# Attention products on four 32-row strips: float32r parts in place of bf16 parts, four products handed out at a time

## The reference, cut to what matters

```python
# first attention: keys and values from a stride-2 depthwise convolution over the tokens
q = x @ q_w.T + q_b                       # 512 rows
xd = conv(x, stride 2) + conv_b           # 256 rows
k = xd @ k_w.T + k_b; v = xd @ v_w.T + v_b
att = softmax(einsum('bhnd,bhmd->bhnm', q, k) * scale)
out = einsum('bhnm,bhmd->bhnd', att, v)
...
# the others, 512 by 512
att = einsum('bhqd,bhkd->bhqk', q, k) / np.sqrt(D)
att = jnp.where(causal, att, -jnp.inf)
att = softmax(att); out = einsum('bhqk,bhkd->bhqd', att, v)
```

## Time and profile before

| | |
|---|---|
| median of 3 runs | 1876.41 us (1875.72 to 1876.76) |
| profiled execution, span from first to last instruction | 1910.5 us |
| time of the profiled execution around its span | not recorded |
| PE / DVE / ACT / POOL busy | 81% / 68% / 51% / 56% of the span |
| attention block that is not causal (units 0 to 31) | about 140 to 410 us |
| causal block of 8 batches | about 546 to 843 us in full swing |
| causal block of 16 batches | about 1064 to 1690 us |

### The profile page before, as it was taken

One profiled execution on the slowest core, in us unless ns is written; L12 is line 12 of the kernel. 1 busy time (PEld: TensorE's weight loads), 2 busy tenths in 40 slices (PEclk: granted clock), 3 DMA queues, 4 the chain that ended last, 5 costly groups with the idle time before them and its releaser, 6 DMA issues. The chain is left out here.

```text
span 1910.5 us, 46442 instructions
## 1 busy us (share of the span) xinstructions
PE 1556.0 (81%) x17682; PEld 947.9 (50%) x17682; DVE 1307.4 (68%) x3414; ACT 968.9 (51%) x2039; POOL 1077.0 (56%) x1712
## 2 busy tenths in 40 slices
PE   5548888885599998885899499999999999866992
PEld 5432333344355554543677255555555555435772
DVE  7348897883588887766321588888888787775224
ACT  4124667652256676552233166777777766531331
POOL 3436767514467857654354376465566767552552
PEclk9966999987689999886799599999999999975996
DMA  8442323212533222210353343233232223102445
GB/s 279 128 127 86 109 70 95 78 30 83 146 99 115 91 82 78 88 36 22 99 152 102 117 128 105 79 94 103 79 114 82 83 92 103 47 26 62 148 123 160
DMA packets 233187, 188.24 MB, mean 99 GB/s; under 512 B 30035, under 2 KB 221306, under 8 KB 232326
## 3 DMA queue, kind: packets, MB, share of 16 engines
q1 hardware_dynamic: 222582, 166.36, 29.1%
q0 software_dynamic: 10240, 18.89, 3.1%
q10 hardware_dynamic: 144, 0.00, 0.0%
HBM read 104.34 MB, written 80.74 MB: 97 GB/s over the span
## 5 line engine op out<-in xcount | busy, mean ns | idle before, releaser
L1015 DVE TENSOR_REDUCE mx<-PS 128x2 f32<-128x512 f32 (+3 forms) x1408 | 784.3, 612 | 193.2 <-PE PS L653 138.2
L865 ACT ACTIVATE pt<-PS 128x512 f32<-128x512 f32 (+2 forms) x1408 | 669.6, 537 | 311.5 <-PE PS L653 227.9
L670 PE MATMUL PS<-ka,qa 52*128 52x256 bf16 (+3 forms) x2048 | 467.0, 307 | 67.1 <-DVE mx L1015 49.3
L786 PE MATMUL PS<-qa,ka 55*128 55x512 bf16 (+3 forms) x1792 | 462.2, 322 | 33.6 <-DMA qa<-nm 26.5
L730 PE MATMUL PS<-pt,vs 128*32 128x512 f32 (+3 forms) x3584 | 353.1, 484 | 3.7 <-issue 3.0
L653 PE MATMUL PS<-mask_q,identh 64*128 64x64 bf16 x3072 | 301.3, 193 | 0.7 <-issue 0.7
L653 PE MATMUL PS<-mask_k,identh 64*128 64x64 bf16 x3072 | 299.6, 192 | 0.5 <-issue 0.5
L786 PEld LDWEIGHTS PS<-qa,ka 55*128 55x128 bf16 x1792 | 167.6, 94 | 262.6 <-issue 102.7
L653 PEld LDWEIGHTS PS<-mask_k,identh 64*128 64x128 bf16 x3072 | 250.2, 97 | 51.1 <-issue 6.6
L653 PEld LDWEIGHTS PS<-mask_q,identh 64*128 64x128 bf16 x3072 | 254.3, 98 | 30.2 <-issue 8.2
L670 PEld LDWEIGHTS PS<-ka,qa 52*128 52x128 bf16 x2048 | 172.8, 95 | 98.1 <-DVE mx L1015 61.2
(11 more groups left out here) (249 smaller groups left out, 2353.2 us busy)
## 6 DMA issues: line engine op xcount, KB each, us to landing
pt<-in_f_w SPq DMA_DIRECT2D x96, 256.0 KB
qa<-q_parts SPq DMA_DIRECT2D x256, 96.0 KB
ka<-k_parts SPq DMA_DIRECT2D x192, 96.0 KB
q_parts<-parts SPq DMA_DIRECT2D x32, 384.0 KB, 3.0
k_parts<-parts SPq DMA_DIRECT2D x24, 384.0 KB, 2.6
xn<-y_rows SPq DMA_DIRECT2D x32, 256.0 KB, 3.2
hid<-y_rows SPq DMA_DIRECT2D x32, 256.0 KB, 3.5
q_parts<-parts SPq DMA_DIRECT2D x32, 256.0 KB, 3.1
```

The source lines that it names most:

```text
L670: mm = pe.matmul(PS[:, bank, i * n:(i + 1) * n], k.qa[rows, b % 2, g, h // 2, qb * P:(qb + 1) * P], k.ka[rows, b % 2, g, h // 2, 0:n], sta ...
L786: mm = pe.matmul(PS[:, bank, i * n:(i + 1) * n], k.ka[rows, b % 2, g, h // 2, kb * P:(kb + 1) * P], k.qa[rows, b % 2, g, h // 2, q0:S], st ...
L865: nc.scalar.activation(k.pt[:, u % 2, at[c]:at[c] + len(heads) * n], PS[:, SC_BANK + c % RING, 0:len(heads) * n], ACT.Exp, scale=SCORE_SCA ...
L1015: nc.vector.tensor_reduce(out, PS[:, MX_BANK + t % RING, 0:len(heads) * n] .rearrange("p (h n) -> p h n", n=n), AX.X, ALU.max).then_inc(s. ...
```

## The change

- Parts: queries and keys are split into two parts, the first rounded to float32r and the second the rest in float32. Three products of parts are summed. With a spare row for each feature that makes 4 times 8 = 32 rows, one strip of the array, one head a strip. The negative maximum goes into two of the spare rows, in two parts, so `put_max` has two DMAs and `max_split` two POOL steps where there were four; `split` has two where there were four. All four heads of a unit sit on the four strips of one tile.
- Hand-out: `slots` issues two score tiles and two max tiles together, on four different strips, after their waits; then second pieces, and then their masks, strip by strip. Its semaphore increments come with the last mask.
- Masks: a diagonal square gets four 32-row products of 32 columns, 64 on each side in a unit (32 before), in bf16 as before. The step rows are gone.
- Tiles: a causal unit still has 12 and 12. The score tiles are 4 of 512, 4 of 384 and 4 of 256 + 128 columns of one head; the max tiles are 4 of 512, 4 of 384 + 128 and 4 of 256. The 384 + 128 tile is reduced in blocks of 128, so one small reduction per unit is added on DVE, and `max_T` waits for it (`mx_ready`).
- Order: inserted work stands behind odd slots alone, `max_T` and `nm` behind slot 1, `value_p` behind slot 3, and the others are dealt out anew.
- The loads of a unit are one DMA for queries and one for keys (two each before), 32-bit data in rows of 2 KB.

```diff
-NPROD = 6
-Q_ROWS = (slice(0, 6, 2), slice(1, 6, 4), slice(3, 4))
-K_ROWS = (slice(3, 6), slice(1, 3), slice(0, 1))
...
+STRIP = P // HG
+DROWS = STRIP // D
+Q_ROWS = (slice(0, 3, 2), slice(1, 2))
+K_ROWS = (slice(1, 3), slice(0, 1))
+SPARE = 3
+MAX_ROWS = (SPARE, SPARE + DROWS)
+WRITES = 2
+MASKS = P // STRIP
...
-        chunks = ([(0, (h,), 512) for h in (0, 1, 2, 3)] + [(1, (h,), 384) for h in (0, 1, 2, 3)]
-                  + [(kb, heads, S - kb * P) for kb in (2, 3) for heads in ((0, 2), (1, 3))])
-        maxes = ([(3, (h,), 512) for h in (1, 0, 3, 2)] + [(2, (h,), 384) for h in (1, 0, 3, 2)]
-                 + [(qb, heads, (qb + 1) * P) for qb in (1, 0) for heads in ((1, 3), (0, 2))])
-        when = {"value_p": 2, "max_T": 2, "o_out": 2, "nm": 2, "o_T": 5, "value0": 8, "x_T": 8, "k": 5, "ctx_T": 8,
-                "q": 11, "v": 11, "out": 5, "value1": 11, ...
+        chunks = ([(h, ((0, 0, 512),)) for h in heads] + [(h, ((1, 0, 384),)) for h in heads]
+                  + [(h, ((2, 0, 256), (3, 256, 128))) for h in heads])
+        maxes = ([(h, ((3, 0, 512),), 512, 3) for h in other_heads]
+                 + [(h, ((2, 0, 384), (0, 384, 128)), P, 0) for h in other_heads]
+                 + [(h, ((1, 0, 256),), 256, 1) for h in other_heads])
+        when = {"max_T": 1, "nm": 1, "value_p": 3, "o_out": 3, "ctx_T": 5, "x_T": 5, "k": 5, "value0": 7, "f_T": 7,
+                "v": 9, "out": 9, "q": 9, "value1": 11, ...
+        o_T_slot = (9, 5)
...
+            def slots(u, i, scores=True, ahead=2):
+                more = u + ahead < U
+                for c in (i - 1, i):
+                    if scores:
+                        score_wait(u, c)
+                        score_piece(u, c, 0)
+                    if more:
+                        max_wait(u + ahead, c)
+                        max_piece(u + ahead, c, 0)
+                for c in (i - 1, i):
+                    if scores and len(chunks[c][1]) == 2:
+                        score_piece(u, c, 1)
+                    if more and len(maxes[c][1]) == 2:
+                        max_piece(u + ahead, c, 1)
+                for n in range(2 if causal else 0):
+                    for j in range(MASKS):
+                        for c in (i - 1, i):
+                            if scores and n < len(chunks[c][1]):
+                                score_mask(c, n, j)
+                            if more and n < len(maxes[c][1]):
+                                max_mask(c, n, j)
...
+                mm = pe.matmul(PS[:, SC_BANK + c % RING, col:col + n],
+                               k.ka[rows, b % 2, g, kb * P:(kb + 1) * P].bitcast(F32R),
+                               k.qa[rows, b % 2, g, q0:S].bitcast(F32R), start=(i == 0), stop=(last and not causal))
...
+                mm = pe.matmul(PS[:, SC_BANK + c % RING, first:first + STRIP], k.key_at[rows, j, :],
+                               k.key_masked[rows, :], start=False, stop=last)
...
+                if causal and t == NMX - 1:
+                    dve.wait_ge(*s.max_taken.at(u * NMX + BLOCK_MAXES))
+                    nc.vector.tensor_reduce(k.mx[:, u % 2, 3, :, 2], k.mx[:, u % 2, 0:3, :, 0].rearrange("p r h -> p h r"), AX.X, ALU.max)\
+                        .then_inc(s.mx_ready.h, 1)
...
-                pool.tensor_copy(hi, full).then_inc(s.nm_hi.h, 1)
-                pool.wait_ge(*s.nm_hi.at(u + 1))
-                pool.tensor_tensor(rest, full, hi, ALU.subtract).then_inc(s.nm_rest.h, 1)
-                pool.wait_ge(*s.nm_rest.at(u + 1))
-                pool.tensor_copy(mid, rest).then_inc(s.nm_mid.h, 1)
-                pool.wait_ge(*s.nm_mid.at(u + 1))
-                pool.tensor_tensor(lo, rest, mid, ALU.subtract).then_inc(s.nm_ready.h, 1)
+                pool.tensor_copy(hi.bitcast(F32R), full).then_inc(s.nm_hi.h, 1)
+                pool.wait_ge(*s.nm_hi.at(u + 1))
+                pool.tensor_tensor(lo, full, hi, ALU.subtract).then_inc(s.nm_ready.h, 1)
```

More of the change, by code:

```diff
@@ L558, in attention @@
+        last_front = (11, 9, 11, 3, 9, 11)
         early, late = ((0,), (1,)), (2, 3)
     else:
[L560 to L564, removed]
@@ L565, in attention @@
-        last_front = (7, 5, 7, 3, 6, 7)
+        chunks = [(h, ((kb, 0, 512),)) for kb in range(KB) for h in heads]
+        maxes = [(h, ((qb, 0, nk), (qb + 1, nk, nk)), nk, qb) for qb in range(0, TB, 2) for h in other_heads]
+        when = {"max_T": 1, "nm": 1, "value_p": 3, "o_out": 3, "ctx_T": 3, "x_T": 3, "k": 5, "value0": 7, "f_T": 7,
+                "v": 7, "out": 5, "q": 5, "f_l": 7, "moments": 3, "f_moments": 3,
+                "late0": 0, "late2": 4, "late_root": 0, "choose": 5, "ranks": 5, "find": 6, "mark": 6, "f_rows": 0}
@@ L571, in before @@
+    BLOCK_MAXES = max(i for i in range(NMX) if maxes[i][2] == P) + 1 if causal else 0
     def before(u, i, n):
@@ L608, in order @@
                       if i > NB - 2 - FIRST - FRONT_LAG]
[L609 to L615, removed]
-            events += [("q", b + 2)]
-        if g == 3 and b + 2 < NB:
-            events += [("k", b + 2)]
-        events += [(f"value{i}", u) for i in range(len(early))]
         if r.sent:
@@ L631, in order @@
                 plan.append(("max", i))
-            out_early = last_front[1] - 2 if b == NB - 1 else when["out"]
-            plan += [(name, n) for name, n in events if (out_early if name == "out" else when[name]) == i]
+            for name, n in events:
+                slot = when[name] if name != "o_T" else o_T_slot[n % 2]
+                if early_out and name in ("ctx_T", "out"):
+                    slot = {"ctx_T": 9, "out": 5}[name]
+                if slot == i:
+                    plan.append((name, n))
             plan += [(name, n) for name, n, slot in fronts if slot == i]
@@ L648, in take_misc, with score_wait @@
                     pe.wait_ge(*misc[0][0].at(misc[0][1]))
-            def mask(bank, col, half, table):
-                for j in range(2):
-                    own = slice(j * HALF, (j + 1) * HALF)
-                    mm = pe.matmul(PS[:, bank, col + j * HALF:col + (j + 1) * HALF],
-                                   k.identh[half * HALF:(half + 1) * HALF, j, :],
-                                   table[half * HALF:(half + 1) * HALF, j, own], start=False, stop=(j == 1))
-                return mm
+            def score_wait(u, c):
+                if c == 0:
+                    pe.wait_ge(*s.m_landed[u % G].at(32 * (u // G + 1)))
+                if before(u, c, NCH) > 0:
+                    pe.wait_ge(*s.pt_ready.at(before(u, c, NCH)))
@@ new lines, in score_piece, with max_piece @@
+                if last and not causal:
+                    mm.then_inc(s.sc_full.h, 1)
+            def max_piece(u, t, i):
+                b, g = u // G, u % G
+                h, pieces = maxes[t][0:2]
+                qb, col, n = pieces[i]
+                rows, last = slice(h * STRIP, (h + 1) * STRIP), i == len(pieces) - 1
+                mm = pe.matmul(PS[:, MX_BANK + t % RING, col:col + n],
+                               k.qa[rows, b % 2, g, qb * P:(qb + 1) * P].bitcast(F32R),
+                               k.ka[rows, b % 2, g, 0:n].bitcast(F32R), start=(i == 0), stop=(last and not causal))
+                if last and not causal:
+                    mm.then_inc(s.max_full.h, 1)
@@ L819, in _ @@
                     if name == "score":
-                        slot(u, n)
+                        if n % 2:
+                            slots(u, n)
                     elif name == "max_T":
@@ L1008, in max_tile @@
             def max_tile(u, t):
-                qb, heads, n = maxes[t]
+                h, pieces, n, first = maxes[t]
+                groups = sum(piece[2] for piece in pieces) // n
                 dve.wait_ge(*s.max_full.at(u * NMX + t + 1))
@@ L1296, in _ @@
                 load_results(sp, k, i)
-            for half in range(2):
-                row = half * HALF + ROWS
-                sp.dma_start(k.qa[row:row + TB, :, :, :, :].rearrange("r b g s t -> r (b g s) t"),
-                             k.q_steps[:, causal, :].unsqueeze(1).to_broadcast([TB, 4 * G, S])).then_inc(s.steps_landed.h, 16)
             for side in range(2):
```

321 lines of the change are left out of this document (151 added, 170 removed).

## The result

The changed kernel takes 2018.53 us (median of 4 runs, 2011.35 to 2020.81) against 1876.59 us: ratio 1.0745, 95% interval 1.0725 to 1.0766. It is 7.5% slower, where 1853 us was forecast, and outside the range.

What follows compares the result with a forecast made beforehand. The prediction took the loop of the maxima to bound the first block, PE and DVE in turn the causal units. Its terms -24 + 6 - 5 = -23 us, from the median 1876.4, gave 1853 us, range 1808 to 1928.

Steps and rivals of the forecast that it cites:

- The failed step: the clock: PE: with half the main columns gone, 1.2 GHz more often; each 0.05 costs 20 to 30 us, about 1880; chance 0.03.
- The loop no longer binds: First block: the loop of the maxima shortens to 5.0 us, DVE binds next; 6.7 us a unit for 7.59, -24 us.
- Causal units: Causal blocks: PE's added work and pairs against evened gaps, +6 us for 96 units (0.06 each), bounds -0.35 and +0.5.
- the prediction's other case: Causal units, weight loads before pairs: if fast weight load held for float32r, 0.03 us for 0.11, giving 2.96 us a unit.
- the evened order: Causal blocks: inserted work evened out, no gap over one job of 1.1 us; set against pairs waiting for two tiles.
- Pairs starve DVE and ACT: Second max tile of every pair: DVE idles in each of six pairs, +0.5 us a unit, +48, 1895 us; chance 0.19.
- Block starts: Three block starts: split loses a cast, a subtraction and a write, loads half their issues; 1.7 us each, -5 us.
- float32r like float32: Main products: float32r streams at two cycles a column, +0.2 us for each of six pairs, +77, 1940 us; chance 0.12.
- strips that don't overlap: Causal masks on strips: small products don't overlap, each costs 0.03 us, +2.3 a unit, +220, 2070 us; chance 0.02.

Runs made afterwards that it cites:

- the order alone: Kernel before with only the changed kernel's order of inserted work (and its added wait on `fm_ready`): 1853.75 us, ratio 0.9892; again 1856.21 us.
- pairs on halves: Kernel before with the changed order of work, plus tiles handed out in pairs, four main products on the two halves, then both tiles' masks: 1879.62 us, ratio 1.0014.
- bf16 on strips: Changed kernel with main products on the upper halves of the float32r words read as bf16: 1920.43 us, ratio 1.0224.
- tile by tile: Changed kernel with tiles handed out one at a time, masks included: 2587.29 us, ratio 1.3756; with first pieces of main products issued twice, 3025.39 us.
- 64-row-mask run: Changed kernel, float32r kept, with masks of 64 rows and 64 columns, two a piece in place of four: 2023.0 us, ratio 1.0790.
- run of 34 rows: Kernel before with the changed order of work, main products over the first 34 of their 52 and 55 rows: 1868.48 us, ratio 0.9959.

## Why the prediction was wrong

From the order alone to the changed kernel in steps, each by the three windows (at the full clock, and what the low clock adds): pairs +46 and -1 us; strips and small masks -52 and +69; float32r +61 and +28. The sum is +55 and +95, all against the order alone, which itself took 21 us from the median. The step called strips and small masks holds the new tiles, loads and splits too, and it brings 12 of the 15 us at the block starts, which lie outside the windows (60 us for the three starts with pairs on halves, 72 with bf16 on strips).

- **The failed step: the clock.** The forecast's sum had no term for it. A rival named it ("with half the main columns gone it may stand at 1.2 GHz more often"), with a chance of 0.03 and a price of "20 to 30 us" for each 0.05. The clock fell by 0.054 and cost 84 us. The price was too low because it counted 3% of PE's busy time in one block, which is 17 us and not even the 20 to 30 that it states. The reason it gave is borne out in part: with the main products doubled in pairs the low time fell from 337 to 211 us, but tile by tile doubling them left the clock down, and fewer rows at the same columns lowered it too. A unit at 1.2 GHz takes 14.1 to 15.1 us in place of 9.5 to 10, as PE, then the bound, has all its work slowed.
- **"The loop no longer binds": true, and not worth -24 us.** The wait on the DMA fell from 26.5 to 7.1 us, but the first block came to 7.43 us a unit at the full clock where 6.7 was taken; DVE was put at 6.2 with gaps guessed. No run got below 7.0. That is -11 us at the full clock; the low clock added 29, so the block grew by 19. The same placement without the rest gave nothing for the transpose alone.
- **Causal units: +0.06 forecast, +0.20 and +0.36 measured,** 29 us for 94 intervals in place of 6, within the bounds of +0.5. The single prices held: columns in 0.23 us, bare load 0.10, strips side by side. The type cost 0.53 and 0.79 a unit, where six bare loads at 0.10 are 0.60, so a load of 0.03 us, the prediction's other case, is out. What failed is the balance: the prediction set the evened order against the pairs and kept nothing. Alone the order gained 0.33 and 0.23 us a unit, and the pairs on it lost 0.49 and 0.46.
- **Pairs starve DVE and ACT** (0.19, +0.5 us a causal unit): the size is as forecast, 0.46 to 0.49 alone, and the place is not. It was to be the second max tile of every pair, waiting for DVE. In the changed kernel it is mostly the second score tile of one pair in six, which waits 0.56 us for ACT. In the sum the strips' gain hides part of it.
- **Block starts: -5 forecast, +15 measured.** POOL's split did lose two steps, but the path to the first transpose ran through the load of the keys, which took 6.4 us to its first product in place of 2.8, and through the first unit's maxima, 9.8 us in place of 7.1 (7.1 with pairs on halves, 8.6 with bf16 on strips). The prediction noted that loads grow from 192 to 256 KB and priced only their issues.
- **float32r like float32, and strips that don't overlap:** rightly dismissed. The first four products of the 64-row-mask run start within 0.01 us. The Trainium skill, TensorE: Matmul & The Clock Gate, section "Wait — 56ns, not 53.3ns?", has starts never closer than about 25 ns; the trace agrees on one strip (1454.66 and 1454.70) and not across strips (1454.66 and 1454.67).
- **Left open:** how much of the strips' 69 us of low clock is rows. The run of 34 rows, with about as many rows in each product as the changed kernel, added 86 to 94 us of low time; strips with bf16 added 145 over pairs. What the rest is, and why tile by tile with float32r it hardly ever recovers, no run separates. The 84, 18 and 15 us (low clock, full clock, block starts) make 117 of the 142; the rest lies outside the windows, or in the slow profile of before, and is not traced further.

The Trainium skill, TensorEngine Tiling (Array Packing), section "PSUM Bottleneck", warns that after a fourfold speed-up of TensorE the copying out of PSUM may become the bound. The trace agrees only in part: PE's loads wait 219.5 us for an exponential, most of it beside other work of PE, but ACT is busy for 48% of the span and itself idle 421.6 us before its exponentials. So where PE is held up, it is by the three banks of a ring and not by the rate of reading.

## What to carry to other kernels

Price a cut in TensorE's work at both levels of its clock: take from the trace what a unit costs wholly at 1.2 GHz and how long it stands there, and ask whether the cut leaves the array emptier; here the time at the low clock was most of the loss, though not all of its cause is known. Handing out two tiles at once cost time on a ring of three banks. Price the loads at the start of a block as well as the work that they feed. And try the order of work by itself first: it was the only part that lowered the time.

## What the runs showed of the hardware

- PE can be busy for 99.8% of 1049 us by the profile and be held at 1.2 GHz for 960 of them, with two float32r products of 32 rows at a time.
- With the same instructions, products over 34 rows in place of 52 and 55 doubled the time at 1.2 GHz (81 and 89 to 175 us).
- A 64-row product waits until 32-row products have drained, on whichever rows they lie, and the other way round: 0.43 against 0.33 us to the first mask, and strict alternation of 0.54 us a product and its masks at 1.2 GHz.
- A float32r product streams its columns as fast as bf16 does (512 in 0.23 us); its bare weight load costs 0.10 us more, at 512 and at 256 columns.
